# Routed tiles in four regions, and their results loaded and added between the tiles

## What is computed

```python
def ffn(x):                                   # x: (2, 1024, 128), used twice
    flat = x.reshape(2048, 128)
    probs = softmax(flat @ router_w.T)        # 8 experts
    topk_p, topk_i = top_k(probs, 2)          # each token goes to 2 experts
    topk_w = topk_p / topk_p.sum(-1)
    out = sum over e: mlp(flat, w_fc[e], w_proj[e]) * combine[:, e]
    return out + mlp(flat, shared_fc, shared_proj)

def attn(x):                                  # a scan over 1024 positions
    k, v = split(x @ W_KV)
    ... 1024 gradient steps on (W1, b1, W2, b2) ...
    return mlp(params, x @ W_Q)

x = x + 0.5 * ffn(layernorm(x))
x = x + attn(layernorm(x))
x = x + 0.5 * ffn(layernorm(x))
```

## Time and profile before

| | us |
|---|---|
| median of 3 runs (466.26 to 467.94) | 466.26 |
| the profiled execution | 466.07 |
| its span, first to last instruction | 464.3 |
| granted TensorE clock, mean share of full speed | 0.946 |
| PE busy, share of the span | 89% |
| DVE, ACT, POOL busy | 59%, 51%, 50% |

### The profile page before, as it was taken

One profiled execution on the slowest core, in us unless ns is written; L12 is line 12 of the kernel. 1 busy time (PEld: TensorE's weight loads), 2 busy tenths in 40 slices (PEclk: granted clock), 3 DMA queues, 4 the chain that ended last, 5 costly groups with the idle time before them and its releaser, 6 DMA issues. The chain is left out here.

```text
span 464.3 us, 9899 instructions
## 1 busy us (share of the span) xinstructions
PE 412.7 (89%) x2859; PEld 331.2 (71%) x2859; DVE 273.3 (59%) x1001; ACT 235.5 (51%) x601; POOL 233.7 (50%) x355
## 2 busy tenths in 40 slices
PE   7899899999934898999999999999999699999930
PEld 5544599999932467888888888866544499999930
DVE  3846445555528667777777777746865245555514
ACT  2495255555530355565555655535794155555510
POOL 4367777554530143546555465550277777454530
PEclk9799999999975999999999999999799899999975
DMA  8981417100026700000000000000011426110028
GB/s 225 260 306 54 115 55 211 38 29 31 10 78 160 193 0 1 3 2 2 1 3 1 2 0 3 1 2 2 0 42 52 116 72 192 33 34 28 16 68 220
DMA packets 34514, 30.90 MB, mean 67 GB/s; under 512 B 3838, under 2 KB 30085, under 8 KB 34464
## 3 DMA queue, kind: packets, MB, share of 16 engines
q1 hardware_dynamic: 24608, 19.17, 15.1%
q0 software_dynamic: 4544, 8.47, 5.6%
q10 hardware_dynamic: 5312, 2.62, 2.1%
HBM read 15.55 MB, written 15.61 MB: 67 GB/s over the span
## 5 line engine op out<-in xcount | busy, mean ns | idle before, releaser
L1719 DVE TENSOR_TENSOR sq<-bank,relu 128x512 f32<-128x512 f32 x86 | 59.4, 691 | 85.4 <-ACT relu L846 85.1
L1469 POOL DMA_INDIRECT y_dram<-y_out,stage x78 | 76.8, 984 | 59.5 <-ACT y_out L872 52.7
L748 PE MATMUL bank<-proj_w,sq 128*128 x624 | 86.4, 281 | 2.9 <-DVE sq L1719 2.8
L735 PE MATMUL bank<-tileT,tile_w 128*128 128x128 f32 x624 | 83.2, 277 | 0.0
L1464 POOL DMA_INDIRECT slots_dram<-rows,slots x64 | 63.4, 990 | 35.5 <-issue 14.9
L748 PEld LDWEIGHTS bank<-proj_w,sq 128*128 128x128 f32 x624 | 75.6, 191 | 6.5 <-issue 3.8
L846 ACT ACTIVATE relu<-bank 128x512 f32<-128x512 f32 x94 | 56.0, 595 | 46.2 <-PE bank L735 37.7
L735 PEld LDWEIGHTS bank<-tileT,tile_w 128*128 128x128 f32 x624 | 77.0, 195 | 0.0
L872 ACT ACTIVATE y_out<-bank,stage 128x128 f32<-128x128 f32 x78 | 28.6, 367 | 33.4 <-PE bank L748 33.4
L1331 POOL TENSOR_TENSOR sq<-sq,guess_rows 128x128 f32<-128x128 f32 x33 | 14.1, 427 | 46.1 <-DVE sq L1302 46.1
L696 PE MATMUL bank<-ln_t,fc_w 128*128 128x512 f32 x64 | 34.4, 636 | 0.0
(11 more groups left out here) (278 smaller groups left out, 946.2 us busy)
## 6 DMA issues: line engine op xcount, KB each, us to landing
slots_dram<-pad SPq DMA_DIRECT2D x2, 2535.0 KB, 13.9
stage<-slots_dram SPq DMA_DIRECT2D x18, 260.0 KB, 4.6
fc_w<-experts SPq DMA_DIRECT2D x1, 2048.0 KB, 20.5
proj_w<-experts SPq DMA_DIRECT2D x1, 2048.0 KB, 23.9
stage<-y_dram SPq DMA_DIRECT2D x8, 256.0 KB, 5.4
stage<-y_dram ACTq DMA_DIRECT2D x8, 256.0 KB, 6.0
y_dram<-y_out,stage POOLq DMA_INDIRECT x78, 2.3
res<-x SPq DMA_DIRECT2D x4, 256.0 KB, 4.0
```

The lines of the kernel that those rows point to most:

```text
L735: last = nc.tensor.matmul(bank[i % 2][:, f_cols], tile_w[:, i % 2, f_cols], tileT[:, (f * NQ + tile_q(i)) % 2, tile_cols(i)], start=True, ...
L748: last = nc.tensor.matmul(bank[4 + i % 2][:, 0:P], sq[:, i % 2, f_cols], proj_w[:, k, f_cols], start=j == 0, stop=j == FJ - 1)
L1469: nc.gpsimd.indirect_dma_start(y_dram.ap(), bass.IndirectOffsetOnAxis(tiles[:, t, P:P + 1].bitcast(U32), 0), y_out[:, t % YBUFS, :], None, ...
L1719: nc.vector.tensor_tensor(wide_of(i)[2], wide_of(i)[0][:], wide_of(i)[1], ALU.mult)\
```

## The change

Four things are changed; line numbers in the diff's new code are those of the changed kernel.

1. **Regions.** Four regions (REGIONS) take the place of two. HALF goes from 9 blocks to 8 and EARLY from 11 tiles to 9. The first region holds full tiles of rows of blocks 0 to 7, the second completes these blocks, the third completes group 2, the fourth group 3. So after tile 22 (23 tiles) all results of groups 0 and 1 are made, after tile 30 those of group 2 (ROWS_BY = 23, 23, 31, 39). The first tile group has one tile instead of three, and the early tiles are groups 0 to 2 (1, 4, 4). There are 11 tile groups, 10 result buffers.
2. **Loads.** `load_results` loads one group and one choice and waits for the scatters of that group's tiles only. In pass 1 all eight loads stand on SP; in pass 2 SP has all but one, with the stores of finished groups between them.
3. **Adds.** `beside_tile` puts the adds of groups 0 to 2 behind the square and the weight copy of tiles 29 to 32, 37 and 38. In pass 1 it adds the parameter casts at tile 20, the statistics of groups 0 and 1 at tiles 33 and 34, their moments at 35, a first guess of the roots at 36, and the statistics of group 2 at tile 38.
4. **Roots in pass 1.** They are refined on POOL (`pool_refined`, 12 small operations, each waiting for the one before) for groups 0 and 1 together behind the scatter of tile 35, for group 2 behind the first key cast, for group 3 inside the second first step. DVE waits for them (`rstd_done`) before each normalisation; group 3 is added within the first step of the scan. PE no longer keeps itself busy there. `k_rows` and `kk` get memory of their own.

```diff
-HALF = NBLK // 2 + 1
+HALF = NBLK // 2
 EARLY = HALF * TOPK - E + 1
+REGIONS = 4
+ROWS_BY = tuple(TOPK * GRP * max(g + 1, HALF // GRP) + E - 1 for g in range(NG))
...
+        def pool_refined(pool, at, n, c):
+            y, z, half = rs_y[:, c], rs_z[:, c], rs_h[:, c]
+            pool.wait_ge(guess_made, 2 * n)
+            for _ in range(3):
+                pool_link(pool, nc.gpsimd.tensor_tensor(z, y, y, ALU.mult), at)
+                pool_link(pool, nc.gpsimd.tensor_tensor(z, z, half, ALU.mult), at)
+                pool_link(pool, nc.gpsimd.tensor_tensor(z, one_half[:, c], z, ALU.subtract), at)
+                last = nc.gpsimd.tensor_tensor(y, y, z, ALU.mult)
+                if _ < 2:
+                    pool_link(pool, last, at)
+            return last
...
-            nt = [1, NWORDS * PER_WORD, 2 * E - 1]
+            nt = [1, NWORDS * PER_WORD, REGIONS * E - 1]
...
-        def load_results(eng, f, k):
+        def load_results(eng, f, g, k):
             for n in range(YBUFS):
-                eng.wait_ge(y_stored[n], 16 * tiles_of_buf(n) * (f + 1))
-            for g in range(NG):
-                eng.dma_start(...).then_inc(y_in[g], 16)
+                eng.wait_ge(y_stored[n], 16 * (tiles_of_buf(n) * f + tiles_of_buf(n, ROWS_BY[g])))
+            eng.dma_start(...).then_inc(y_in[g], 16)
...
             sp_tiles(0)
+            for g in range(NG):
+                for k in range(TOPK):
+                    load_results(sp, 0, g, k)
...
                 for t in range(NT):
                     pool.wait_ge(y_made, f * NT + t + 1)
...
+                    if f == 0 and t == 35:
+                        pool_refined(pool, at, 2, slice(0, 2 * GRP)).then_inc(rstd_done, 1)
...
             pool_tiles(0)
             pool_key_part(pool, 1, 0)
+            pool_refined(pool, at, 3, slice(2 * GRP, 3 * GRP)).then_inc(rstd_done, 1)
...
                 make_slope(nc.gpsimd, pool, step)
+                if step.n == 1:
+                    pool_refined(pool, at, 4, slice(3 * GRP, NBLK)).then_inc(rstd_done, 1)
...
-            load_results(act, 1, 1)
-            store_out(act, 1)
+            load_results(act, 1, 3, 1)
+            store_out(act, 1, 3)
...
+            def beside_tile(f, t):
+                if f == 0 and t == 20:
+                    dve.wait_ge(params_in, 16 * 7)
+                    start_params()
+                if t in (29, 30):
+                    add_routed(f, 0, t - 29)
+                if t in (31, 32):
+                    add_routed(f, 1, t - 31)
+                if f == 0 and t in (33, 34):
+                    stats_of(t - 33)
+                if f == 0 and t == 35:
+                    norm_moments(dve, at, 0, at[0])
+                    norm_moments(dve, at, 1, at[0])
+                if f == 0 and t == 36:
+                    norm_guess(dve, at, slice(0, 2 * GRP))
+                if t in (37, 38):
+                    add_routed(f, 2, t - 37)
+                if f == 0 and t == 38:
+                    stats_of(2)
...
             tiles_of(0)
-            dve.wait_ge(params_in, 16 * 7)
-            start_params()
-            stats_there = add_routed(0, True)
-            for g in range(NG):
-                norm_moments(dve, at, g, stats_there)
-            norm_scale(dve, at)
+            dve.wait_ge(rstd_done, 2)
             normalise(dve, 0)
             normalise(dve, 1)
+            norm_moments(dve, at, 2, at[0])
+            norm_guess(dve, at, slice(2 * GRP, 3 * GRP))
...
             for step in first_steps():
-                dve_key_part(dve, *key_part(5 * step.n))
-                if step.n < 2:
-                    normalise(dve, 2 + step.n)
+                if step.n == 2:
+                    dve.wait_ge(rstd_done, 4)
+                    normalise(dve, 3)
                 dve_aa(dve, step)
-                dve_key_part(dve, *key_part(5 * step.n + 1))
+                if step.n == 0:
+                    dve.wait_ge(rstd_done, 3)
+                    normalise(dve, 2)
+                elif step.n == 1:
+                    norm_moments(dve, at, 3, at[0])
+                    norm_guess(dve, at, slice(3 * GRP, NBLK))
                 dve_u(dve, step)
...
                 dve_ee(dve, step)
+                if step.n == 0:
+                    add_routed(0, 3, 0)
+                    add_routed(0, 3, 1)
...
-            pe.wait_ge(res_done, NG // 2)
-            pe_keep_busy(5)
-            pe.wait_ge(res_done, NG)
-            pe_keep_busy(3)
+            pe.wait_ge(y_made, NT)
```

More of the change, by code:

```diff
@@ L520, in route @@
-            late, early = n_tiles[:, 0, :], n_tiles[:, 1, :]
-            dve_link(dve, nc.vector.tensor_tensor(late, n_tiles[:, 2, :], early, ALU.subtract), at)
-            dve_link(dve, nc.vector.tensor_tensor_scan(
-                tile_ends[:, 1:2 * E + 1], ones[:, 0:2 * E], n_tiles[:, 0:2, :].rearrange("p h e -> p (h e)"), 0.0, ALU.mult,
-                ALU.add), at)
-            early_start = tile_ends[:, E:2 * E]
-            dve_link(dve, nc.vector.tensor_scalar(early_start, early_start, tile_ends[:, 2 * E:2 * E + 1], float(NT),
-                                                  ALU.subtract, ALU.add), at)
@@ L528, in route @@
-            dve_link(dve, nc.vector.tensor_tensor(late_start[:], tile_ends[:, 0:E], early, ALU.subtract), at)
-            dve_link(dve, nc.vector.tensor_tensor(late_gap[:], late_start[:], early_start, ALU.subtract), at)
+            nc.vector.tensor_copy(count_i[:, 0, :], counts[:, 0, :])
+            dve_link(dve, nc.vector.tensor_scalar(count_i[:, 1:, :], counts, float(P - 1), None, ALU.add), at)
+            dve_link(dve, nc.vector.tensor_scalar(count_i[:], count_i[:], P.bit_length() - 1, None,
+                                                  ALU.logical_shift_right), at)
@@ new lines, in route @@
+            dve_link(dve, nc.vector.tensor_copy(reach[:, 1:, :], count_i[:]), at)
+            dve_link(dve, nc.vector.tensor_tensor(n_tiles[:], reach[:, 1:, :], reach[:, 0:REGIONS, :], ALU.subtract), at)
+            dve_link(dve, nc.vector.tensor_tensor_scan(
+                tile_ends[:, 1:REGIONS * E + 1], ones[:, 0:REGIONS * E], n_tiles[:].rearrange("p h e -> p (h e)"), 0.0,
+                ALU.mult, ALU.add), at)
+            dve_link(dve, nc.vector.tensor_tensor(
+                offset_of[:].rearrange("p h e -> p (h e)"), tile_ends[:, 0:REGIONS * E],
+                reach[:, 0:REGIONS, :].rearrange("p h e -> p (h e)"), ALU.subtract), at)
@@ L632, in pe_counts @@
             pe.wait_ge(upto_done, f + 1)
-            nc.tensor.matmul(bank[6][:, P:P + 2 * E], ones[:], upto[:, :, HALF - 1::NBLK - HALF], start=True, stop=True)
+            nc.tensor.matmul(bank[6][:, P:P + (REGIONS - 1) * E], ones[:], upto[:, :, HALF - 1::GRP], start=True, stop=True)
             by_block = [t[:].rearrange("p e b -> p (e b)") for t in (upto, both)]
@@ L722, in transposed @@
                 for t in group_tiles(q):
-                    last = nc.tensor.transpose(bank[6 + n % 2][:, tile_place(t)], tiles[:, t, 0:P], ident[:])
+                    last = nc.tensor.transpose(bank[6 + n % 2][:, tile_place(t)], tiles[:, tile_at(t), 0:P], ident[:])
                 last.then_inc(tileT_done, 1)
@@ L871, in weighted @@
                     act.wait_ge(y_stored[t % YBUFS], 16 * n)
[L872 removed]
+                nc.scalar.mul(y_out[:, t % YBUFS, :], bank[4 + i % 2][:, 0:P], tiles[:, tile_at(t), P + 1:P + 2])\
                   .then_inc(y_made, 1)
@@ L1387, in _ @@
             sp_tiles(1)
-            store_out(sp, 0)
+            for k in range(TOPK):
+                load_results(sp, 1, 0, k)
+                load_results(sp, 1, 1, k)
+            for g in range(2):
+                for b in range(B):
+                    store_out(sp, b, g)
+            for k in range(TOPK):
+                load_results(sp, 1, 2, k)
+            for b in range(B):
+                store_out(sp, b, 2)
+            load_results(sp, 1, 3, 0)
+            store_out(sp, 0, 3)
             sp.wait_ge(stored, 16 * B * NG)
@@ L1908, in _ @@
             tiles_of(1)
-            add_routed(1, False)
+            for k in range(TOPK):
+                add_routed(1, 3, k)
         @block.tensor
```

199 lines of the change are left out of this document (97 added, 102 removed).

## The result

The changed kernel takes 453.81 us (median of 4 runs, 449.93 to 454.61) against 466.98 us of the kernel before beside it (4 runs, 466.26 to 467.94): a ratio of 0.97, 95% interval 0.964 to 0.976. The prediction was 454.0. The profiled execution took 454.26, with a span of 452.5.

A forecast was written before the change was run, and what follows sets the result against it. PE was taken to bound the tile loops; terms -20.5, +4.9, +3.5, +1.8, +3.3, +0.6 and -5.9 sum to -12.3, from 466.07 to 453.8, stated as 454.0 us. Range about 449 to 459, or 448 to 460.5 with slower POOL refining.

The forecast's parts named there:

- Pass 1, results: End of pass 1: groups 0 to 2 added inside the loop, first key product at 135.9 instead of 156.36, -20.5 us.
- rival B: POOL's refining is much slower beside DVE, in the first steps and at the loop's end: 459 us, chance 0.14.
- First steps: First steps of the scan: PE waits for group 3's late root, +4.9 us, bounds +2.8 and +6.2.
- The clock: Lowered clock behind three PE waits, both tile waits and one in the first steps: 1.1 each, +3.3 us, bounds 0 and 6.
- Tile 9: Tenth tile: PE waits for its rows to be sent and loaded, +3.5 us in pass 1, +1.8 in pass 2.
- Rival A: The tenth tile's rows come in time and PE never stands there: some 443 us, chance 0.08.
- The routing's words: Pass 2, shared expert: routing's last part grows and PE waits for its words; charged nothing, first tiles 2.6 us earlier.
- Between the tiles: Tile loops: added DVE operations just fit into DVE's 0.76 us waits, 0.04 each, +0.6 us, bounds 0 and 2.
- Rival C: Added work does not fit between tiles, all 15 operations delay the square: +9.8 instead of +0.6, 463 us, chance 0.07.
- The end: End of the kernel: only group 3 is left to add, 458.4 instead of 464.3, -5.9 us, between -5 and -6.7.

The follow-up runs named there:

- the second profile: A later profile of the changed kernel itself, unedited, run again beside the last experiments on one chip: 454.69 us, ratio 0.972 to the kernel before.
- both passes late: Changed kernel with both passes' results loaded and added behind the tiles, regions and routing as changed: 479.93 us, ratio 1.030 to the kernel before.
- a second operation: Changed kernel with one more unread DVE operation of the same size beside each add of groups 0 to 2: 457.93 us, ratio 0.982.

## Why the prediction was right, step by step

**Pass 1, results.** Forecast -20.5, measured -20.2 and -20.6 in the two profiles. POOL's refining is what the normalisation waits for, as forecast. It took 4.1 us instead of 3.6, with rival B's mechanism in small; three rows of the changed kernel's timeline:

```profile
135.94 0.68 DVE L1807 TENSOR_TENSOR res<-res,stage 128x512 f32<-128x512 f32 x1
136.09 0.59 POOL L463 TENSOR_TENSOR rs_y<-rs_y,rs_z 128x8 f32<-128x8 f32 x1
136.76 0.20 POOL L460 TENSOR_TENSOR rs_z<-rs_y 128x8 f32<-128x8 f32 x1
```

An operation of 0.20 takes 0.59 when it starts beside an add; two of the twelve do, so B costs under 1 us. The Trainium skill (SBUF — State Buffer, SBUF: two separate sides) says that a VectorE operation with two inputs in SBUF and a GpSimd operation that reads SBUF take turns at a shared port pair for whole instructions; by that rule POOL's operation waits for the add, which reads `res` and `stage`, to end, and the trace agrees: 135.94 + 0.68 and 136.09 + 0.59 end within 0.06 us of each other.

**First steps.** Forecast +4.9 and 1.1 of clock; measured +8.6 in the first profile and +6.4 in the second. The waits were right: PE's transposes for group 3 stand 21.22 us behind the first key product instead of 14.00, and 2.35 of the 7.22 are the clock at the end of pass 1, which leaves 4.87. That this meets +4.9 so closely is luck: DVE's operation for the slope of step 1 (156.02) came 1.66 later and not 2.1, and from it to the transposes it was 6.04 and not 5.6. The clock was the term that was mis-sized: 1.4 behind the wait, not 1.1, and in the first profile 2.35 for key products at 1.2 GHz (5.58 us from the first key product to the first step's product, 3.23 before). I charged no clock to that place; the second profile shows none. That POOL's refining alone makes this wait was only partly right: 1.6 of it goes with the refining, 2.0 stays behind DVE's mask product.

**Tile 9.** Rival A fell: PE waits in both passes, for the load, as forecast. Pass 1: forecast 3.5 and 1.1, measured 2.5 and 1.4 (3.89 in all); I had PE ready at 67.6, and it was at 68.5, so the waits of 2.25 and 2.52 stayed under the 3 to 5 that I had named. Pass 2, from the counts to tile 9: forecast 1.8 and 1.1, measured 2.99, of which 1.45 clock. The second profile has 4.6 and 3.7, with waits of 2.94 and 4.62.

**The routing's words.** They are late. DVE casts them at 335.08, and the square that PE needs stands behind them; PE and the clock, in the changed kernel's profile:

```profile
335.93 1.12 PE L721 MATMUL bank<-sq,proj_w 128*128 128x512 f32 x2 [2.13 <-DVE stage L1756]
337.00:341.00 4.00, 4.00 (x10) 2.13 (x9) 1.82 (x5) 1.37 (x3) 3.09 (x4) 0.58 0.20 66
```

So tile 0 comes 34.74 us behind the counts, 0.4 earlier than before and not the 2.6 that I wrote. As I argued, this costs nothing, since tile 9 waits for POOL's sends anyway. In the second profile PE waits 0.92 for that square, tile 0 comes 1.2 earlier, and the wait for tile 9 takes it back (4.62 us).

**Between the tiles.** Forecast +0.6, measured 0.5 in both passes together (0.49 + 0.41, less 0.2 each for the transposes). No add between the tiles waited for its load. Rival C fell; twice the operations cost 2.5.

**The end.** Forecast -5.9, measured -6.65, the bound. Both loads together land sooner: the first add starts 3.62 us behind their issue, 4.03 before. The Trainium skill (DMA: Bandwidth & Descriptors, Anatomy of one DMA) gave an estimate of 3.2, by a fit that the page gives for transfers issued from GpSimd, while these are issued from SP and ACT; the measurement is in between and decides.

**What I had not forecast.** The scan to the counts of pass 2 is 1.65 shorter, in a stretch that the change does not touch. Its last part, before and after, in the columns of the clock's stretches above:

```profile
326.00:330.00 4.00, 4.00 (x9) 2.32 (x10) 3.53 (x40) 1.59 (x4) 2.15 (x10) 0.50 0.00 0
318.00:322.00 4.00, 3.61 (x14) 1.82 (x14) 3.83 (x48) 2.58 (x5) 2.70 (x13) 1.00 0.01 4
```

In the profile of before the clock is at its lower level there, in the changed kernel's at its upper one. Two later profiles with the same scan take 155.10 and 155.39 us again, so this gain is chance and not the change's. It and the end's 0.75 make up for the 2.6 in the first steps: the sum was right to half a microsecond (-11.8 between the spans against -12.3) in part by luck, because errors of 2.6 and 2.4 cancelled.

## What to carry to other kernels

When a batch is made smaller so that its results can be used earlier, look where the next batch's load is waited for in PE's program, and move that place behind work that is already there: here two tiles' work covered the whole wait. A long pause of PE cost twice here, once itself and once at the lower clock behind it; products that nobody reads bought back the second part where they left a pause of 1.76 us or less, and did not where they left 2.12 or 2.97. Before moving the head of a chain through three engines, ask where its middle stands in line: group 3's adds came 4.9 us earlier (6.13 behind the first key product instead of 11.04), its transposes 0.3.

## What was not expected of the hardware

The same program lowered the clock at the end of pass 1 in one profile and not in the other (key products of 2.08 and 1.12 us). Of the experiments' profiles, the four of one chip (group 3's adds moved, its root not refined, both passes late, a second operation) have the slow products, and the four of another do not. Two of the first four and three of the second have the same pauses of 0.46, 0.74 (0.75) and 0.68 us; both passes late has 19.67 and the second operation 1.35 in place of 0.74, and one of the second four fills them. What sets them apart is open. Nor did the clock fall behind long pauses alone: at the end of the scan it fell in the profile of before, where PE's longest pause in the 10 us ahead was 0.69, and stayed up in the changed kernel's behind the same pause. The time from POOL's 32nd send to the landing of tiles 9 to 12 varied from 5.0 to 6.3 us between profiles, which moves tile 9 by as much as some of the edits do; a stretch of the table says more about an edit than the median where that happens.
